# A selective-scan block on one core: B's bf16 split on TensorE and ScalarE, u formed from PSUM in one step per half, its overflow guard on GpSimd, and the units written out

## The reference

```
u = silu(causal_conv(u_raw, 4 taps) + conv_b)             # 256 features
dt_low, B, C = split(u @ x_proj_w.T)                      # 8, 16 and 16 columns
dt = softplus(dt_low @ dt_proj_w.T + dt_proj_b)
for every token t:  h = exp(dt*A) * h + (dt*u) * B        # 16 states per feature
                    y = sum over the states of h * C
y = (y + u*D) * silu(z)
```

## Time and profile before

| | |
|---|---|
| median of three runs | 1336.19 us (1335.76 to 1339.44) |
| the profiled execution | 1343.07 us, of which the span of instructions is 1341.3 us |
| granted TensorE clock, mean | 0.94 |
| busy: DVE, PE, POOL, ACT | 90%, 82%, 81%, 58% of the span |

### The profile page before, as it was taken

The page is one execution under the profiler, slowest core; times in us unless marked ns, Lnnn a source line. Parts: engine busy times, 40 slices in busy tenths (PEclk is TensorE's granted clock), DMA queues, the critical chain, the costliest instruction groups (busy, mean ns, idle before and its releaser), DMA issues.

```text
span 1341.3 us, 16943 instructions
## 1 busy us (share of the span) xinstructions
PE 1094.4 (82%) x3770; PEld 641.5 (48%) x3770; DVE 1211.3 (90%) x1440; ACT 779.3 (58%) x1423; POOL 1089.0 (81%) x699
## 2 busy tenths in 40 slices
PE   6687888887887887877877877977977888877997
PEld 4343454444444544544544534534534544533887
DVE  1499999999999999999999999999999999999761
ACT  2465665666666666666666656656656656656230
POOL 3288799798898888898898898898897998987850
PEclk9688988999989989989989989989989989888999
DMA  6221221222221221221221222212212213214361
GB/s 155 73 96 48 99 85 68 77 96 78 77 96 62 93 96 54 94 101 55 94 88 67 96 69 86 95 55 100 95 55 100 96 55 116 94 56 140 110 179 30
DMA packets 64537, 116.64 MB, mean 87 GB/s; under 512 B 34218, under 2 KB 47954, under 8 KB 64466
## 3 DMA queue, kind: packets, MB, share of 16 engines
q1 hardware_dynamic: 64466, 115.96, 25.4%
HBM read 108.47 MB, written 7.47 MB: 86 GB/s over the span
## 4 chain that ended last, share of the span: by engine, by line
DVE 44%; issue 21%; PE 18%; ACT 11%; DVEq 3%; POOL 2%; DMA 0%; ACTq 0%; POOLq 0%; SPq 0%
DVE SCAN L936 26%; DVE SCAN L887 8%; PE Yp L672 4%; ACT DA L480 4%; DVE GATES L922 3%; PE PP L701 3%; PE PP L751 3%; POOL SCAN L412 2%; PE PP L716 2%; PE PP L784 2%; DVE VV L898 2%; DVE UDT L1015 2%; DVE GATES L1038 1%; ACT GATES L563 1%; DVE X L1022 1%
## 5 line engine op out<-in xcount | busy, mean ns | idle before, releaser
L412 POOL TENSOR_TENSOR SCAN<-SCAN,CS 128x768 f32<-128x768 f32 x384 | 695.1, 1824 | 99.8 <-DVE SCAN L936 94.3
L936 DVE TENSOR_TENSOR_SCAN SCAN<-DA,CAR,SCAN 128x384 f32<-128x384 f32 x768 | 728.5, 995 | 4.6 <-ACT DA L480 4.0
L672 PE MATMUL Yp<-SCAN,IDENT 128*128 128x384 f32 x1536 | 594.9, 513 | 145.5 <-DVE VV L898 75.8
L480 ACT ACTIVATE DA<-UDT,A 128x384 f32<-128x384 f32 x768 | 442.9, 582 | 446.6 <-DVE SCAN L936 443.6
L672 PEld LDWEIGHTS Yp<-SCAN,IDENT 128*128 128x128 f32 x1536 | 288.5, 198 | 352.2 <-issue 139.5
L887 DVE TENSOR_TENSOR SCAN<-UDT,BB 128x768 f32<-128x768 f32 x288 | 269.0, 934 | 26.8 <-PE BB L654 16.1
L420 POOL TENSOR_TENSOR SCAN<-UDT,BS 128x768 f32<-128x768 f32 x96 | 175.5, 1828 | 0.0
L818 PE MATMUL PP<-XN,WT 128*128 (+1 forms) x384 | 141.8, 505 | 0.2
L654 PE MATMUL BB<-PT,SEL 96*128 96x384 bf16 x288 | 96.6, 336 | 20.3 <-DVE SCAN L887 20.3
L436 POOL TENSOR_TENSOR UDT<-UDT 128x768 f32<-128x768 f32 x24 | 43.4, 1809 | 76.4 <-DVE UDT L1042 76.4
L818 PEld LDWEIGHTS PP<-XN,WT 128*128 128x128 f32 x384 | 73.4, 196 | 59.8 <-issue 16.4
(11 more groups left out here) (156 smaller groups left out, 1130.7 us busy)
## 6 DMA issues: line engine op xcount, KB each, us to landing
CS<-bc_rows SPq DMA_DIRECT2D x96, 768.0 KB, 4.0
BS<-bc_rows SPq DMA_DIRECT2D x24, 768.0 KB, 5.9
out<-XN SPq DMA_DIRECT2D x32, 192.0 KB, 2.5
X<-in_x SPq DMA_DIRECT2D x24, 192.0 KB, 3.4
X<-in_L_ffn_memory_tokens SPq DMA_DIRECT2D x16, 256.0 KB, 3.2
XN<-in_L_ffn_memory_tokens SPq DMA_DIRECT2D x16, 256.0 KB, 3.1
bc_rows<-XDT SPq DMA_DIRECT2D x24, 48.0 KB, 1.5
X<-in_L_ffn_memory_router SPq DMA_DIRECT2D x1, 512.0 KB, 3.5
```

The lines of the kernel that those rows point to most:

```text
L412: pool.tensor_tensor(M[:, n1 % MRING], HB[:, n1 % HRING], over_halves(CS[:, n1 % CRING]), ALU.mult).then_inc(m_ready, 1)
L480: act.activation(DA[:, h, 0:T], DT[:, par, h], ACT.Exp, scale=A[:, h, n:n + 1])\
L672: last = pe.matmul(Yp[:, h, 0:T], IDENT[:, :], M[:, n3 % MRING, h], start=n3 == 0, stop=n3 == NS - 1)
L936: dve.tensor_tensor_scan(HB[:, s % HRING, h], DA[:, h, 0:T], HB[:, s % HRING, h], CAR[:, ds(J * NS * HALVES + s * HALVES + h, 1)], ALU.mul ...
```

## The change

```diff
@@ constants and buffers
+EXP_LIMIT = 1.0e19
-        LESS = sb("LESS", [DTROW, PARTS - 1])
+        LESS = sb("LESS", [DTROW, PARTS - 1, DTROW], BF16)
+        NCB = sb("minus_conv_bias", [P, HALVES])
@@ run_units (all compute engines) and SP's loop
-            with eng.Fori(1, (UNITS - 4) // 2) as i:
+            for i in range(1, (UNITS - 4) // 2):
                 unit(2 * i, 0)
                 unit(2 * i + 1, 1)
-            with sp.Fori(0, CHUNKS - 1) as c:
+            for c in range(CHUNKS - 1):
@@ POOL step, after M of s - 1
+                if front and s == 0:
+                    pool.wait_ge(sg_chain, 2 * f + 1)
+                    pool.tensor_scalar(SG[:, :, :], SG[:, :, :], EXP_LIMIT, 0.0, ALU.min, ALU.max).then_inc(clamped, 1)
@@ ACT weights
+                act.activation(NCB[:, :], CB_[:, :], ACT.Copy, scale=-1.0)
@@ ACT step, before the decays
-                if front and s == 1:
-                    act.wait_ge(clamped, 2 * f + 2)
-                    positive(act, u_ready, f)
-                    act.activation(SG[:, :, :], U[:, fp], ACT.Exp, scale=-1.0).then_inc(sg_chain, 1)
-                if front and s == 6:
+                if conv and s == 15:
+                    act.wait_ge(conv_ready, 2 * (J + 2) + 1)
+                    positive(act, u_ready, J + 2)
+                    act.activation(SG[:, 0], PP[:, 0, 0:T], ACT.Exp, bias=NCB[:, 0:1], scale=-1.0)
+                if front and s == 0:
+                    act.wait_ge(conv_ready, 2 * f + 2)
+                    act.activation(SG[:, 1], PP[:, 1, 0:T], ACT.Exp, bias=NCB[:, 1:2], scale=-1.0).then_inc(sg_chain, 1)
+                if front and s == 5:
                     act.wait_ge(res_ready, f + 1)
                     act.activation(PART[:, :], PP[0:DTROW, 1, 0:T], ACT.Copy).then_inc(mid_ready, 1)
+                if front and s == 6:
+                    act.wait_ge(res2_ready, f + 1)
+                    act.activation(PT[:, fp], PP[0:DTROW, 1, 0:T], ACT.Copy).then_inc(parts_ready, 1)
@@ ACT step, after the decays
                 if front and s == 1:
-                    act.wait_ge(sg_chain, 2 * f + 1)
+                    act.wait_ge(clamped, f + 1)
                     act.activation(SG[:, :, :], SG[:, :, :], ACT.Ln, bias=1.0).then_inc(sg_chain, 1)
                 if front and s == 2:
                     act.wait_ge(sg_chain, 2 * f + 2)
-                    act.activation(PPT, SG[:, :, :], ACT.Exp, scale=-1.0).then_inc(sg_ready, 1)
+                    act.activation(SG[:, :, :], SG[:, :, :], ACT.Exp, scale=-1.0).then_inc(sg_ready, 1)
@@ PE step, at its end, before the dt projection
+                if front and s == 4:
+                    if at(J, -1):
+                        pe.wait_ge(less_set, 2)
+                    pe.wait_ge(hi_ready, f + 1)
+                    pe.matmul(PP[0:DTROW, 1, 0:T], LESS[:, 0], PART[:, :], start=False, stop=False,
+                              skip_group_check=True).then_inc(res_ready, 1)
+                if front and s == 5:
+                    pe.wait_ge(mid_ready, f + 1)
+                    pe.matmul(PP[0:DTROW, 1, 0:T], LESS[:, 1], PART[:, :], start=False, stop=True,
+                              skip_group_check=True).then_inc(res2_ready, 1)
@@ DVE weights: LESS becomes two 96x96 bf16 matrices, made once from IDENT
+                for part in range(1, PARTS):
+                    rows = slice(part * BC, (part + 1) * BC)
+                    for step in range(part):
+                        last = dve.tensor_scalar(LESS[rows, step], IDENT[rows, 0:DTROW], -1.0, None, ALU.mult)
@@ DVE step
-                if front and s == 6:
-                    dve.wait_ge(hi_ready, f + 1)
-                    dve.scalar_tensor_tensor(out=PP[0:DTROW, 1, 0:T], in0=PART[:, :], scalar=LESS[:, 0:1],
-                                             in1=PP[0:DTROW, 1, 0:T], op0=ALU.mult, op1=ALU.add)
                 if front and s == 3:
-                    dve.wait_ge(clamped, 2 * f + 2)
                     dve.wait_ge(sg_ready, f + 1)
-                    dve.tensor_tensor(U[:, fp], U[:, fp], PPT, ALU.mult).then_inc(u_ready, 1)
+                    for h in range(HALVES):
+                        last = dve.scalar_tensor_tensor(out=U[:, fp, h], in0=PP[:, h, 0:T], scalar=CB_[:, h:h + 1],
+                                                        in1=SG[:, h], op0=ALU.add, op1=ALU.mult)
+                    last.then_inc(u_ready, 1)
-                if front and s == 0:
-                    for h in range(HALVES):
-                        dve.wait_ge(conv_ready, 2 * f + h + 1)
-                        dve.tensor_scalar(U[:, fp, h], PP[:, h, 0:T], CB_[:, h:h + 1], NEG_LIMIT, ALU.add, ALU.max)
-                if front and s == 6:
-                    dve.wait_ge(mid_ready, f + 1)
-                    dve.scalar_tensor_tensor(out=PT[:, fp], in0=PART[:, :], scalar=LESS[:, 1:2],
-                                             in1=PP[0:DTROW, 1, 0:T], op0=ALU.mult, op1=ALU.add)
```

More of the change, by code:

```diff
@@ L106, in build @@
         A = sb("A", [P, HALVES, NS]); AE = sb("AE", [P, HALVES, NS])
-        CB_ = sb("conv_bias", [P, HALVES]); DV = sb("DV", [P, HALVES])
+        CB_ = sb("conv_bias", [P, HALVES]); NCB = sb("minus_conv_bias", [P, HALVES]); DV = sb("DV", [P, HALVES])
         CW = sb("CW", [P, HALVES, TAPS])
@@ L163, in build @@
         sg_ready = sem("sg_ready"); u_ready = sem("u_ready"); xp_ready = sem("xp_ready")
-        hi_ready = sem("hi_ready"); res_ready = sem("res_ready"); mid_ready = sem("mid_ready")
+        hi_ready = sem("hi_ready"); res_ready = sem("res_ready"); res2_ready = sem("res2_ready"); mid_ready = sem("mid_ready")
         parts_ready = sem("parts_ready"); dtp_ready = sem("dtp_ready"); sp_chain = sem("sp_chain")
@@ L856, in weights @@
                     dve.tensor_scalar(DD[:, h], IDENT[:, :], DV[:, h:h + 1], None, ALU.mult)
-                dve.memset(LESS[:, :], 0.0).then_inc(less_set, 1)
+                dve.memset(LESS[:, :, :], 0.0).then_inc(less_set, 1)
                 dve.wait_ge(less_set, 1)
-                dve.memset(LESS[BC:2 * BC, 0:1], -1.0)
-                dve.memset(LESS[2 * BC:3 * BC, :], -1.0).then_inc(less_set, 1)
-                dve.wait_ge(less_set, 2)
+                for part in range(1, PARTS):
+                    rows = slice(part * BC, (part + 1) * BC)
+                    for step in range(part):
+                        last = dve.tensor_scalar(LESS[rows, step], IDENT[rows, 0:DTROW], -1.0, None, ALU.mult)
+                last.then_inc(less_set, 1)
             X0v = X[:, 0:BATCH * T].rearrange("p (b q t) -> p q b t", b=BATCH, q=Q)[:, :, :, 0]
@@ L904, in step @@
                         drive(J + 1, 1 - par, 0, N + 1)
-                if front and s == 6:
-                    dve.wait_ge(hi_ready, f + 1)
-                    dve.scalar_tensor_tensor(out=PP[0:DTROW, 1, 0:T], in0=PART[:, :], scalar=LESS[:, 0:1],
-                                             in1=PP[0:DTROW, 1, 0:T], op0=ALU.mult, op1=ALU.add)\
-                        .then_inc(res_ready, 1)
                 if back and s == 10:
@@ L1010, in step @@
                     weigh(3)
-                if front and s == 0:
-                    for h in range(HALVES):
-                        dve.wait_ge(conv_ready, 2 * f + h + 1)
-                        dve.tensor_scalar(U[:, fp, h], PP[:, h, 0:T], CB_[:, h:h + 1], NEG_LIMIT, ALU.add, ALU.max)\
-                            .then_inc(clamped, 1)
                 if back and s == 5:
@@ L1023, in step @@
                     last.then_inc(x2_ready, 1)
-                if front and s == 6:
-                    dve.wait_ge(mid_ready, f + 1)
-                    dve.scalar_tensor_tensor(out=PT[:, fp], in0=PART[:, :], scalar=LESS[:, 1:2],
-                                             in1=PP[0:DTROW, 1, 0:T], op0=ALU.mult, op1=ALU.add)\
-                        .then_inc(parts_ready, 1)
                 if main and s == 11:
```

## The result

The changed kernel takes 1307.28 us (median of 4 runs, 1306.40 to 1309.15) against 1336.42 us (also of 4) of the kernel before on the same chip: ratio 0.977, 95% interval 0.974 to 0.979. The forecast was 1309. The profiled execution took 1307.87 us with a span of 1306.1.

What follows compares the result with a forecast made beforehand. DVE bounds now, POOL's chain 1.4 us behind; after the change POOL's chain binds at 49.97 us a unit. Inner units 22.1 and edge units 6.5 saved, start +1.0: -27.6 us, giving 1309 us, range 1300 to 1330.

Steps and rivals of the forecast that it cites:

- a second chain: POOL's queue of 30.96 us, then DVE's 18.83, together 49.8 a unit, hidden 1.4 us behind DVE's queue.
- The guard: Min/max step moved into POOL's queue once a unit: 0.90 us, bounds 0.75 and 1.81, estimated from L393.
- Rivals A: Guard on POOL costs as much as a two-input step, 1.81 us: +19, so 1328 us; chance 0.15.
- C: Guard on POOL dearer than any ordinary step there; at 2.8 us the sum is 1349, slower; chance 0.07.
- The hand-over: Alternating PE matmuls and ACT copies of the split: cost nothing; without DVE's wait for POOL some 0.4 us a unit.
- Rival B: PE-ACT hand-over decides, making scan 6 late by 1.7 us: +15, so 1324 us; chance 0.10.
- DVE's new steps: Two 128x384 steps on DVE, 0.53 us each, 1.06 together, at full speed beside POOL; doubling would add 1.06.
- Writing out: Loops unrolled: branch's 0.7 us a unit goes on DVE; POOL's queue 30.62 us instead of 30.96.
- Rival D: Written-out code does nothing or less, POOL's queue stays 30.96: +7, 1316 us; chance counted within the forecast's 0.63.
- The five edge units: Units J = 0, 1, 20, 21, 22, which have a front: 1.3 us gained each, 6.5 in all.
- The start: Unit 0, where the guard comes behind POOL's building of the selectors: start +1.0 us.
- taking the same difference off: Profiled execution was 6.9 us above the median, so 27.6 was subtracted from the 1336.2 median to give 1308.6.

Runs made afterwards that it cites:

- the split-only kernel: Kernel before with units written out and the split of B moved to PE and ACT, no guard: 1305.11 us, ratio 0.975.
- the last kernel: Changed kernel with rows 5, 7, 9 early, projection and B(10) ahead in PE's step 7, means ahead of the sum in step 9: 1282.28 us, ratio 0.959.
- three reorderings: Changed kernel with rows 3, 5, 7, 9 early: 1336.40 us; only 5, 7, 9 early: 1335.95; the latter with PE's step 7 reordered: 1312.97.
- the rolled one: Changed kernel with both hardware loops back and the guard's wait on an added one-element POOL step: 1323.44 us, ratio 0.989.
- early rows and PE reordered: Changed kernel with rows 5, 7, 9 early and PE's step 7 issuing projection and B(10) ahead of the sum: 1312.97 us, ratio 0.980.

## Why the prediction was right

**The bound.** The step that carried it was that a second chain lay close behind DVE. The 1.4 us were read in one unit; over 18 the slack ahead of scan 9 is 1.15, and it goes with PE's clock: 0.35 to 0.38 in the eight units at 1.00, 1.38 to 2.14 in the ten others. The chain became the bound, with its parts as given: queue 31.43 us for 30.62 + 0.90 = 31.52; release and DVE's rest 0.03 + 18.30 for 0.07 + 18.38; unit 49.77 for 49.97. The doubled and the missing guard show the mechanism. Without its waits DVE needs 49.77 - 1.73 - 0.03 = 48.01 us a unit (forecast 47.96): it was relieved of 3.19, its waits included, and 1.43 arrived. Its busy time fell by 45.6 us in all (forecast about 50).

**The guard**: 0.79 us for 0.90, nearest to the lower end of 0.75; L393's 0.87 was 0.08 off, the upper bound of 1.81 far. Rivals A and C fell with it.

**The hand-over**: costed at nothing. PE's two matmuls ran when the projection ended, and DVE waited 0.01 us a unit for a decay. Rival B fell. That it would cost some 0.4 us without the cover of DVE's wait for POOL is not borne out: in the split-only kernel, where that wait is 0.14, decay and B take 0.11 + 0.34, but written out without the split they take more, 0.18 + 0.44; and in the last kernel, where the wait for POOL is 0.31, no wait for a decay shows.

**DVE's new steps**: 1.14 us for the two, beside a working POOL, where two of the old L1015 took 1.11; so not doubled. By the Trainium skill (SBUF — State Buffer, Who interferes with whom) a DVE step with at most one SBUF input, outside the two-port modes, does not contend with GpSimd. The trace agrees: the 48 steps take 0.606 to 0.621 us each.

**Writing out**: on POOL 30.65 us without the guard for 30.62. Rival D fell: by itself the part gives 0.992.

**Where the sum was off.** It came to -27.6 us. The profiled executions differ by 1343.07 - 1307.87 = 35.2. Of this the inner units are 18 x 1.43 = 25.7 (forecast 22.1: guard, release and rest each a little cheaper). The five edge units gained 9.7 where I took 6.5; 3.9 of it came in J = 22, in which one small step of the routing took two very different times:

```profile
1189.59 1.78 DVE L982 TENSOR_TENSOR SQ<-SQ 128x16 f32<-128x16 f32 x1
```

```profile
1158.20 0.16 DVE L1007 TENSOR_TENSOR SQ<-SQ 128x16 f32<-128x16 f32 x1
```

The first fence is DVE's timeline in the kernel before, the second in the changed one: the same step, 1.62 us apart. POOL of the kernel before, at that time:

```profile
1189.52 1.81 POOL L420 TENSOR_TENSOR SCAN<-UDT,BS 128x768 f32<-128x768 f32 x1
```

DVE's small step begins 0.07 us behind it and ends at 1191.37, when POOL's has ended (1191.33). In the changed kernel it begins at 1158.20, between two POOL steps. Where the other 2.3 us of J = 22 come from is open. The start came 1.1 us later (forecast 1.0), and the tail 1.0 us shorter, which I had not. The medians differ by 29.1 only, because the profile of before lay 6.9 us above the median known then and that of after 0.6 above its own: taking the same difference off was the term that failed, by 6.3 us, and it nearly cancelled the 7.6 by which the sum was too small. So the forecast of 1309 owes its last few microseconds to luck. The unit of the changed kernel, 49.97 for 49.77, does not. What it gained is less sure: the 51.20 come from an execution slower than every other one of that kernel here (1335.3 to 1342.0), and what a unit takes in a usual one no trace shows.

What the prediction had not seen is how little each part is worth beside the others: the split and the loop alone reach 1305, and the step with the guard adds nothing to them. Whether it pays once the orders are altered too is argued, not shown, since no run has those orders without it: DVE less its waits is 48.77 us a unit with the split alone, and the last kernel takes 48.52.

## What to carry to other kernels

Before a saving on the busiest engine is costed, look for the ring that runs through the second one: take its queue between two hand-overs, add what the busiest engine does from the step that needs the queue's last result to the one that starts the queue again, and compare with the unit. Only the difference can arrive, plus what the change takes out of the ring itself and less what it adds there. Here 1.4 us of 3.2 arrived; that this equals the slack read in one unit is chance, since the guard's 0.79 was added and some 1.1 went out with the register work, the branch and the wait for the means. Take the mean of many units, and look at each kind: here the slack was 0.4 us in one kind and 1.4 to 2.1 in the other. When the order of a queue is then altered, follow each step that is pushed back through the next in-order queue that reads it: three reorderings here only showed the next wait, and the fourth brought the gain, since each trace had named the instruction behind which the late one stood.

## What the runs showed of the hardware

A two-input step on GpSimd takes 1.81 us for 768 fp32 elements a partition, a one-input step with two constants 0.82. No run has that step with one operation, so what the second one costs is not shown. A loop's branch leaves DVE idle for 1.24 to 1.43 us in the kernel before and for 1.46 to 1.60 in the rolled one. The loop lengthens POOL's queue as well, whichever engine bounds: 31.16 us against 30.62 before, 32.09 (with the small step) against 31.43 after. A two-input DVE step of 16 elements took 1.78 us when it met a two-input POOL step at its begin and 0.16 when it fell between two. It is the same step in every kernel here: in seven it took 0.25 to 1.80 us and ended 0.03 to 0.04 us behind the POOL step under way, in six it took 0.15 or 0.16. Where the line lies is open, since the last one, with early rows and PE reordered, took 1.85 us although it began 0.02 us ahead of POOL's step, as steps of 0.15 did elsewhere:

```profile
1161.77 1.85 DVE L1009 TENSOR_TENSOR SQ<-SQ 128x16 f32<-128x16 f32 x1
```

PE's L687 and L716 took 2.92 and 2.76 us behind a pause of 4.54 us, at a granted clock of 0.50, about double the 1.45 that matmuls of that size take elsewhere. Behind that pause the stretch had 0.50 to 0.55 in all 18 inner units of that kernel; behind the 2.78 us of the changed kernel it had 1.00 in six of 18 and 0.50 to 0.66 in the others. A late product can so cost PE twice.
